# Re-ordering the seam between attention and state-space stage, and handing a block's floor from VectorE to ScalarE

## The chip, the core and the metric

One core of a Trainium2 chip runs the whole kernel in one launch. The metric is the device time of the kernel in microseconds (us). Engines are called by their short names where rows are meant: PE (TensorE), DVE (VectorE), ACT (ScalarE), POOL (GpSimd), SP (SyncE, which here only issues transfers).

## What is computed

Input `x` has 8 sequences of 512 rows and 256 columns. Layer 0 is attention with 16 heads and rotary positions (residual added), then a mixture of 16 experts with capacity 320. Layer 1, the stage in question, is a Mamba block followed by a linear layer whose input and weight are rounded to a 6-bit grid in groups of 32:

```python
xz = in_proj(x); x, z = split(xz)            # 512 inner channels
u = silu(conv4(x) + b)
dt_low, B, C = split(x_proj(u))
delta = softplus(dt_proj(dt_low) + dt_b)     # step sizes
dA = exp(delta * A); dBu = delta * B * u     # 16 states a channel
h = dA * h + dBu; y = sum(h * C)             # along 512 positions
out = out_proj((y + u * D) * silu(z))
scale = max(max|block of 32| / 7.5, tiny)    # grid of the linear layer
```

## The kernel before, in words

`route_block` chooses experts, `attend_block` does attention and the experts for one sequence after another, and `mix_block` does layer 1. All engines meet at a barrier between two of these; the **seam** here is the stretch from the barrier ahead of `mix_block` to its first scans.

In `mix_block` a **block** is one sequence (b, or f while it is being prepared, 0 to 7). Its work is 32 **steps** (n counts them over all blocks, q within one), eight to each of four chunks c of 128 channels. A step has two halves m = 2n and 2n + 1. For each half ACT writes the decays exp(delta * A) into one of five banks of PSUM (`decay`, L1447), POOL writes the drives of both halves to one of eight places in `work` (`drive`, L1325), DVE runs the recurrence in the bank (`scan`, L1554) and then multiplies the state by C (`read`, L1560), and PE sums the states of two steps (`sum_states`, L1657). So DVE's order is scan, read, scan, read, and ACT and POOL can be at most some steps ahead of it.

Step sizes reach the decays through memory: ACT takes delta out of PSUM (`take_dt`, L1410 and L1411), then softplus as an exponential (L1415) and a logarithm (L1419); POOL finishes them (`scale_input`, L1310 to L1314); SP stores them (`store_inputs`, L1214) and loads them back spread to 128 partitions (`load_inputs`, four transfers, L1224; the first two let the first step begin, the other two the second). B and C come the same way (`store_rows` L1202, `load_quad` L1209).

While block b is scanned, block f = b + 1 is prepared: each part stands at a fixed step, by the tables `PE_AT`, `ACT_AT`, `DVE_AT`, `POOL_AT` (steps counted from the start of block f - 1's steps, negative ones before it). On DVE these parts are the `statistics` and `aggregate` of the normalisation (L1517, L1524), `block_max` (L1531), the largest magnitude in each group of 32, and `block_scale` (L1535 floors it, L1537 takes its reciprocal). Everything that DVE does for them stands between two scans.

Block 0's front part runs inside `attend_block`. What is left of it at the seam (step sizes, z, the transposed constants, the linear layer's weight) and the normalising of block 1 run before the loop over steps.

## Time and profile before

| | us |
|---|---|
| median of 3 runs (lowest to highest) | 2017.42 (2014.82 to 2017.91) |
| the profiled execution: its own time | 2016.76 |
| its span in the trace | 2015.0 |
| barrier ahead of `mix_block` | 1044.6 |
| first scan starts | 1073.80 |
| last scan starts | 2003.2 |

Times inside the trace count from the span's start. In the rows further down an arrow in brackets gives the idle time before an instruction and what ended it. "L1554" is a line of the kernel before.

### The profile page before, as it was taken

Reading aid. Unit: us, or ns where it says so; the run is one execution under the profiler, and the core shown is the slowest. Engines: PE = TensorE matmul, PEld = TensorE weight load, DVE = VectorE, ACT = ScalarE, POOL = GpSimd, SP = SyncE. Lnnn points to the kernel's source line nnn. Section 1 sums busy time; section 2 is a strip of 40 time slices with the busy share of each in tenths; the row PEclk is TensorE's granted clock in tenths of the full one; section 3 lists DMA queues with packets and bytes.
Section 4 is the critical chain, followed back from the end, with each engine's and each line's share of the span. In section 5 each row is a group of like instructions: output and inputs, shape, how many; then the busy total and the mean of one; then the engine's idle time right before and its main releaser. Section 6 shows DMA issues by size and latency. Waiting matters only on the chain. (4 is left out here: it accounts for less than half of the span.)

```text
span 2015.0 us, 22043 instructions
## 1 busy us (share of the span) xinstructions
PE 1669.7 (83%) x6616; PEld 744.9 (37%) x6616; DVE 1510.4 (75%) x2254; ACT 1001.1 (50%) x1524; POOL 893.5 (44%) x662
## 2 busy tenths in 40 slices
PE   7399999999999999999978578798887878878466
PEld 7262534436253443525223123333332233323132
DVE  6436464564546466454748999999999999999998
ACT  3125435252533425253465756656575665657542
POOL 2610000000000000000339888888879888786963
PEclk9998989899898989989888688898878889788777
DMA  5573542526364252636225152333415233341520
GB/s 193 198 118 107 84 142 47 96 99 105 106 92 133 55 116 70 106 104 105 91 85 195 56 165 95 125 112 127 149 54 188 95 126 113 119 145 44 177 94 11
DMA packets 103331, 223.83 MB, mean 111 GB/s; under 512 B 12913, under 2 KB 65266, under 8 KB 99554
## 3 DMA queue, kind: packets, MB, share of 16 engines
q1 hardware_dynamic: 100194, 214.70, 38.4%
q0 software_dynamic: 3072, 8.37, 1.3%
q8 instruction: 28, 0.46, 0.1%
q14 instruction: 37, 0.30, 0.0%
HBM read 169.57 MB, written 53.48 MB: 111 GB/s over the span
## 5 line engine op out<-in xcount | busy, mean ns | idle before, releaser
L1325 POOL TENSOR_TENSOR work<-rep,bc 128x1024 f32<-128x1024 f32 x256 | 597.0, 2358 | 141.5 <-PE ps L1657 140.3
L1554 DVE TENSOR_TENSOR_SCAN ps<-ps,work 128x512 f32<-128x512 f32 x512 | 623.8, 1218 | 8.3 <-POOL work L1325 8.3
L1447 ACT ACTIVATE ps<-rep,a_neg 128x512 f32<-128x512 f32 x512 | 347.3, 689 | 335.0 <-DVE work L1560 333.5
L832 DVE TENSOR_REDUCE m<-ps 128x1 f32<-128x512 f32 x512 | 328.4, 686 | 162.1 <-PE ps L967 159.2
L719 ACT ACTIVATE prob<-ps 128x1024 f32<-128x1024 f32 x256 | 257.6, 1021 | 236.8 <-PE ps L991 235.1
L1560 DVE TENSOR_TENSOR work<-ps,bc 128x512 f32<-128x512 f32 x512 | 344.5, 673 | 0.0
L637 POOL TENSOR_TENSOR m_parts<-m,nil 128x16 bf16<-128x16 f32 x32 | 7.1, 222 | 589.5 <-DVE m L832 589.5
L1657 PE MATMUL ps<-work,pick 128*32 128x512 f32 x1024 | 165.1, 723 | 92.8 <-DVE work L1560 92.7
L1632 PE MATMUL ps<-xn_sb,front_w 128*128 128x512 f32 (+1 forms) x448 | 216.3, 637 | 26.3 <-ACT xn_sb L1381 26.3
L967 PE MATMUL ps<-k_st,q_st 96*128 96x512 bf16 x512 | 202.2, 440 | 31.7 <-DVE m L832 24.8
L991 PE MATMUL ps<-q_st,k_st 99*128 99x512 bf16 x512 | 168.9, 428 | 0.6
L933 PE MATMUL ps<-rows_t,front_w 128*128 128x320 f32 x512 | 149.4, 440 | 4.3 <-ACT rows_t L697 4.3
L1002 PE MATMUL ps<-prob,v 128*32 128x512 f32 x1024 | 149.2, 657 | 0.1
L1632 PEld LDWEIGHTS ps<-xn_sb,front_w 128*128 128x128 f32 x448 | 88.1, 203 | 159.6 <-issue 122.4
L967 PEld LDWEIGHTS ps<-k_st,q_st 96*128 96x128 bf16 x512 | 50.4, 101 | 209.7 <-DVE m L832 165.7
L942 PE MATMUL ps<-front_w,hid 128*128 128x256 f32 x512 | 120.8, 384 | 6.0 <-ACT hid_rest L701 6.0
L653 POOL TENSOR_TENSOR att<-att,x_res 128x1024 f32<-128x1024 f32 x8 | 18.8, 2347 | 236.3 <-DVE att L817 236.3
L804 DVE COPY e_out<-ps 128x256 f32<-128x256 f32 x32 | 12.0, 417 | 143.8 <-PE ps L942 143.8
L700 ACT ACTIVATE hid<-ps 128x256 f32<-128x256 f32 x128 | 49.2, 384 | 129.9 <-PE ps L933 129.9
L933 PEld LDWEIGHTS ps<-rows_t,front_w 128*128 128x128 f32 x512 | 97.4, 193 | 41.3 <-ACT rows_t L697 4.7
L942 PEld LDWEIGHTS ps<-front_w,hid 128*128 128x128 f32 x512 | 95.1, 189 | 27.4 <-ACT hid_rest L701 11.3
L1657 PEld LDWEIGHTS ps<-work,pick 128*32 128x32 f32 x1024 | 21.7, 116 | 199.2 <-DVE work L1560 156.0
(206 smaller groups left out, 1995.4 us busy)
## 6 DMA issues: line engine op xcount, KB each, us to landing
rep<-rep_rows SPq DMA_DIRECT2D x128, 512.0 KB, 6.2
front_w<-in_w SPq DMA_DIRECT2D x32, 1024.0 KB, 8.5
bc<-bc_rows SPq DMA_DIRECT2D x32, 512.0 KB, 4.7
rep_rows<-inputs SPq DMA_DIRECT2D x32, 512.0 KB, 5.4
qk_parts<-parts SPq DMA_DIRECT2D x96, 128.0 KB
q_st<-qk_parts SPq DMA_DIRECT2D x96, 128.0 KB, 10.5
k_st<-qk_parts SPq DMA_DIRECT2D x96, 128.0 KB, 11.5
dispatch<-zeros SPq DMA_DIRECT2D x4, 1280.0 KB, 10.6
```

The lines of the kernel that those rows point to most:

```text
L719: nc.scalar.activation(prob[:, n % PB, :, :], ps[:, ST[n % 2]:ST[n % 2] + 2, :], ACT.Exp, scale=SCALE).then_inc(prob_ready, 1)
L832: nc.vector.tensor_reduce(m[:, g % 2, qt, 2 * pair + i:2 * pair + i + 1], ps[:, S0 + i, :], AX.X, ALU.max).then_inc(s_reduced, 1)
L933: x = nc.tensor.matmul(ps[:, HIDE[i] + h % 2, 0:CAP], w1[:, i, k, h * P:(h + 1) * P], rows_t[:, k, :], start=(k == 0), stop=(k == KD - 1))
L942: x = nc.tensor.matmul(ps[:, E_OUT[i], j * DM:(j + 1) * DM], hid[:, h, j * P:(j + 1) * P], w2[:, i, h, :], start=(h == 0), stop=(h == HC - 1))
L967: nc.tensor.matmul(ps[:, S0 + i, :], q_st[0:STACK, h, qt * P:(qt + 1) * P], k_st[0:STACK, h, :], start=True, stop=True).then_inc(s_done, 1)
L991: x = nc.tensor.matmul(ps[:, ST[n % 2] + i, :], k_st[0:STACK + MROWS, h, kt * P:(kt + 1) * P], q_st[0:STACK + MROWS, h, :], start=True, st ...
L1325: nc.gpsimd.tensor_tensor(work[:, n % WS, :, :], rep[:, g % RS, 2 * h:2 * h + 2, 1, :], bc[:, k, 0, :].unsqueeze(1).broadcast_to([P, 2, SE ...
L1447: nc.scalar.activation(state(m), rep[:, g % RS, 2 * h + i, 0, :], ACT.Exp, scale=a_neg[:, c, 2 * h + i, k:k + 1]).then_inc(decay_ready, 1)
L1554: nc.vector.tensor_tensor_scan(state(m), state(m), work[:, n % WS, i, :], 0.0, ALU.mult, ALU.add).then_inc(state_ready, 1)
L1560: nc.vector.tensor_tensor(work[:, n % WS, i, :], state(m), bc[:, k, 1, :], ALU.mult).then_inc(read_ready, 1)
L1632: x = nc.tensor.matmul(ps[:, bank, s:], in_x[:, k, TAPS - 1 - s, c * P:(c + 1) * P], xn_t[:, k, 0:SEQ - s], start=(s == 0 and k == 0), sto ...
L1657: x = nc.tensor.matmul(ps[j * CH:(j + 1) * CH, YB, :], pick[:, :], work[:, n % WS, i, :], start=False, stop=(n % PER_CHUNK >= PER_CHUNK - 2))
```

## The change

It has three parts. **At the seam** the step sizes of chunk 0 go through exponential and logarithm alone, before those of the other three; SP stores B and C's rows first, stores chunk 0's inputs between the second and third load of B and C, and loads the linear layer's weight early under a semaphore of its own; POOL does `scale_input` of chunk 0 first, that of chunk 1 next, and those of chunks 2 and 3 inside the loop after steps 8 and 12; DVE quantises the weight and prepares the taps before the statistics of block 1; the silu of block 0's z (`first_z`, in banks 5 and 4 for its last two chunks) moves behind the decays of step 1, and the normalising of block 1 behind those of step 2. **For block 1** most parts of the preparation stand three steps later (`late`). **In every block** the floor of the group maxima moves from one DVE `tensor_scalar` to three ACT instructions (`floor_max`, step 2), `block_scale` waits for them and stands at step 2 in place of 1, and the statistics stand one step later. The tests `at == X_AT[...]` of block 1's other parts are changed like those shown.

```diff
-Z_FIRST = (6, 7, 0, 1)
+Z_FIRST = (6, 7, 5, 4)
...
-ACT_AT = {"weigh": -15, "normalise": -3, "turned": (0, 0), "x": (4, 6, 8, 10), "round": 5, "silu_u": 11, "quant": (12, 12), "rows": 14,
+ACT_AT = {"weigh": -15, "normalise": -3, "turned": (0, 0), "floor": 2, "x": (4, 6, 8, 10), "round": 5, "silu_u": 11, "quant": (12, 12), "rows": 14,
           "dt": (16, 16, 18, 18), "softplus": 20, "z": (26, 27, 29, 30), "silu_z": 31}
-DVE_AT = {"max": 0, "statistics": -11}
+DVE_AT = {"max": 0, "scale": 2, "statistics": -10}
...
+FIRST_LATE, FIRST_Z, FIRST_ROOT, FIRST_INPUT = 3, 1, 2, (0, 0, 8, 12)
...
+        def late(f):
+            return FIRST_LATE if f == 1 else 0
...
-                    sp.wait_ge(bc_stored, f * 16 + 16)
+                    if f:
+                        sp.wait_ge(bc_stored, f * 16 + 16)
...
+                store_rows(0)
+                sp.dma_start(fw_raw, io["fw"].rearrange("(t p) c -> p t c", p=P)).then_inc(w_loaded, 16)
                 sp.dma_start(a_neg[:, :, :, :], io["a_log"]).then_inc(a_loaded, 16)
...
                 sp.wait_ge(sb["x1_stored"], BATCH * 16)
-                store_rows(0)
+                sp.wait_ge(bc_stored, 16)
                 for k in range(QUADS):
+                    if k == 2:
+                        store_inputs(0, 0)
                     load_quad(0, k)
-                for c in range(DC):
-                    store_inputs(0, c)
-                    if c == 0:
-                        load_inputs(0, 0)
+                load_inputs(0, 0)
                 for b in range(BATCH + 1):
                     if b < BATCH:
                         for c in range(1, DC):
+                            if b == 0:
+                                store_inputs(0, c)
                             load_inputs(b, c)
...
-                        pool.wait_ge(log_ready, f + 1)
+                    if f == 0:
+                        pool.wait_ge(log_ready, min(c, 1) + 1)
+                    elif c == 0:
+                        pool.wait_ge(log_ready, f + 2)
...
-                pool.drain()
+                scale_input(0, 0)
                 add_experts(1)
-                root(1)
-                for c in range(DC):
-                    pool.drain()
-                    scale_input(0, c)
+                scale_input(0, 1)
                 pool.wait_ge(taps_ready, 1)
                 for n in range(BATCH * PIECES):
                     drive(n // PIECES, n % PIECES)
+                    if n == FIRST_ROOT:
+                        root(1)
+                    for c in range(2, DC):
+                        if n == FIRST_INPUT[c]:
+                            pool.drain()
+                            scale_input(0, c)
...
-                        if at == POOL_AT["down"]:
+                        if at - late(f) == POOL_AT["down"]:
...
+                def floor_max(f):
+                    act.wait_ge(max_ready, f)
+                    nc.scalar.activation(absmax[:, :, 0], absmax[:, :, 0], ACT.Copy, scale=GRID_UNIT / GRID_MAX)
+                    act.drain()
+                    nc.scalar.activation(absmax[:, :, 0], absmax[:, :, 0], ACT.Relu, bias=floor[:, 0:1])
+                    act.drain()
+                    nc.scalar.activation(absmax[:, :, 0], absmax[:, :, 0], ACT.Identity, bias=floor[:, 1:2]).then_inc(max_floored, 1)
...
-                def exponents(f):
+                def exponents(f, c0=0):
+                    cs = slice(c0, DC) if f or c0 else slice(0, 1)
                     act.drain()
-                    nc.scalar.activation(du, du, ACT.Exp, scale=-1.0)
-
-                def softplus(f):
+                    nc.scalar.activation(du[:, cs, :], du[:, cs, :], ACT.Exp, scale=-1.0)
+
+                def softplus(f, c0=0):
+                    cs = slice(c0, DC) if f or c0 else slice(0, 1)
                     act.drain()
-                    nc.scalar.activation(du, du, ACT.Ln, bias=1.0).then_inc(log_ready, 1)
+                    nc.scalar.activation(du[:, cs, :], du[:, cs, :], ACT.Ln, bias=1.0).then_inc(log_ready, 1)
...
-                for c in range(DC):
+                def first_z():
+                    for c in range(DC):
+                        act.wait_ge(z_done, c + 1)
+                        nc.scalar.activation(sz[:, 0, c, :], ps[:, Z_FIRST[c], :], ACT.Silu).then_inc(z_taken, 1)
+                    act.drain()
+
+                act.wait_ge(set_up, 1)
+                nc.scalar.activation(idle[:, :], idle[:, :], ACT.Exp)
+                take_dt(0, 0, DT_FIRST[0])
+                exponents(0)
+                softplus(0)
+                for c in range(1, DC):
                     take_dt(0, c, DT_FIRST[c])
                 act.wait_ge(a_loaded, 16)
                 nc.scalar.activation(a_neg[:, :, :, :], a_neg[:, :, :, :], ACT.Exp).then_inc(a_exp, 1)
-                exponents(0)
-                softplus(0)
+                exponents(0, 1)
+                softplus(0, 1)
                 for k in range(KD):
...
+                act.wait_ge(w_turned, 1)
+                nc.scalar.activation(fw_t[:, :, :], ps[:, W_FIRST, :].rearrange("p (k d) -> p k d", d=DM), ACT.Copy).then_inc(w_copied, 1)
...
-                for c in range(DC):
-                    act.wait_ge(z_done, c + 1)
-                    nc.scalar.activation(sz[:, 0, c, :], ps[:, Z_FIRST[c], :], ACT.Silu).then_inc(z_taken, 1)
-                act.wait_ge(w_turned, 1)
-                nc.scalar.activation(fw_t[:, :, :], ps[:, W_FIRST, :].rearrange("p (k d) -> p k d", d=DM), ACT.Copy).then_inc(w_copied, 1)
-                normalise(1)
                 act.wait_ge(a_ready, 1)
                 nc.scalar.activation(idle[:, :], idle[:, :], ACT.Exp)
                 act.drain()
                 for n in range(BATCH * PIECES):
                     b, q = n // PIECES, n % PIECES
                     decay(b, q)
+                    if n == FIRST_Z:
+                        first_z()
+                    if n == FIRST_Z + 1:
+                        normalise(1)
...
-                            if at == ACT_AT["turned"][k]:
+                            if at - late(f) == ACT_AT["turned"][k]:
...
-                        if at == ACT_AT["round"]:
+                        if at - late(f) == ACT_AT["floor"]:
+                            floor_max(f)
...
-                    nc.vector.tensor_reduce(absmax[:, :, 0], blocks(xn[:, :, :]), AX.X, ALU.max, apply_absolute_value=True)
+                    nc.vector.tensor_reduce(absmax[:, :, 0], blocks(xn[:, :, :]), AX.X, ALU.max, apply_absolute_value=True).then_inc(max_ready, 1)
 
                 def block_scale(f):
-                    dve.drain()
-                    nc.vector.tensor_scalar(absmax[:, :, 0], absmax[:, :, 0], GRID_UNIT / GRID_MAX, GRID_UNIT * 1e-30, ALU.mult, ALU.max)
-                    dve.drain()
+                    dve.wait_ge(max_floored, f)
                     nc.vector.reciprocal(inv_scale[:, :], absmax[:, :, 0]).then_inc(scale_ready, 1)
...
+                quantise_weights()
+                tap_weights()
+                dve.wait_ge(a_exp, 1)
+
+                nc.vector.tensor_scalar(a_neg[:, :, :, :], a_neg[:, :, :, :], -1.0, -1e-30, ALU.mult, ALU.min).then_inc(a_ready, 1)
                 statistics(1)
                 aggregate(1)
-                dve.wait_ge(a_exp, 1)
-
-                nc.vector.tensor_scalar(a_neg[:, :, :, :], a_neg[:, :, :, :], -1.0, -1e-30, ALU.mult, ALU.min).then_inc(a_ready, 1)
-                tap_weights()
-                quantise_weights()
...
-                        if at == DVE_AT["max"]:
+                        if at - late(f) == DVE_AT["max"]:
                             block_max(f)
-                        if at == DVE_AT["max"] + 1:
+                        if at - late(f) == DVE_AT["scale"]:
                             block_scale(f)
...
                         pe.wait_ge(y_ready, b * DC + c)
+                    else:
+                        pe.wait_ge(z_taken, DC)
...
+                turn_weights()
                 pe.wait_ge(const_loaded, CONSTS * 16)
...
-                turn_weights()
...
-                pe.wait_ge(xn_ready, 2)
-                for k in range(KD):
-                    turn(k, TB[k], xt_done)
...
-                            if at == PE_AT["turn_x"][k]:
+                            if at == (PE_AT["turn_x"][k] if f > 1 else FIRST_LATE):
...
-                            if at == PE_AT["x"][c]:
+                            if at - late(f) == PE_AT["x"][c]:
```

The first place is SP's queue at the seam. Before, from the second constant on:

```order
L1232 DMA in_z<-in_in_proj_t 128x2x512
L1232 DMA d_par<-in_d_param 128x4
L1232 DMA sz<-in_fw 128x2x256
L1232 DMA pick<-in_pick 128x32
L1232 DMA out_w<-in_out_proj_t 128x1024
L1232 DMA front_rows_w<-in_fbias 1x256
L1202 DMA bc_rows<-front_x_rows 32x512 [waits front_rows_copied,x1_stored]
L1209 DMA bc<-bc_rows 128x1x1024 [waits bc_stored]
L1209 DMA bc<-bc_rows 128x1x1024 x3
L1214 DMA rep_rows<-inputs 128x1024 [waits du_ready]
L1224 DMA rep<-rep_rows 128x1x1024 [waits rep_stored_0]
```

And in the changed kernel, from the barrier on:

```order
L1210 DMA bc_rows<-front_x_rows 32x512 [waits front_rows_copied]
L1237 DMA sz<-in_fw 128x2x256
L1238 DMA a_neg<-in_a_log 128x64
L1243 DMA work<-in_conv_w 128x2048
L1243 DMA in_z<-in_in_proj_t 128x2x512
L1243 DMA d_par<-in_d_param 128x4
L1243 DMA pick<-in_pick 128x32
L1243 DMA out_w<-in_out_proj_t 128x1024
L1243 DMA front_rows_w<-in_fbias 1x256
L1218 DMA bc<-bc_rows 128x1x1024 [waits bc_stored,x1_stored]
L1218 DMA bc<-bc_rows 128x1x1024
L1223 DMA rep_rows<-inputs 128x1024 [waits du_ready]
```

The store of B and C's rows moved from behind all constants to the front of the queue, and the store of the first inputs from behind four loads of B and C to behind two.

The second place is ACT's queue ahead of the first decays (`ps<-rep,a_neg`). Before, from the silu of z on:

```order
L1464 ACT_TABLE_LOAD
L1464 ACTIVATE sz<-ps 128x512 [waits z_done] x4
L1466 ACTIVATE fw_t<-ps 128x512 [waits w_turned]
L1376 ACTIVATE xn_sb<-xn_sb,front_shift,front_rstd 128x256 [waits quant_turned,front_rstd_ready]
L1376 ACTIVATE xn_sb<-xn_sb,front_shift,front_rstd 128x256 x3
L1469 ACT_TABLE_LOAD
L1469 ACTIVATE idle<-idle 128x1 [waits a_ready]
L1447 ACTIVATE ps<-rep,a_neg 128x512 [waits rep_loaded_0_0]
L1447 ACTIVATE ps<-rep,a_neg 128x512
L1381 ACTIVATE xn_sb<-ps 128x512 [waits front_xt_done] x2
L1447 ACTIVATE ps<-rep,a_neg 128x512 [waits rep_loaded_0_1]
```

And in the changed kernel, from the copy of the linear layer's weight on:

```order
L1499 ACTIVATE fw_t<-ps 128x512 [waits w_turned]
L1502 ACTIVATE d_diag<-ident_sb,d_par 128x128 [waits const_loaded3]
L1502 ACTIVATE d_diag<-ident_sb,d_par 128x128 x3
L1505 ACT_TABLE_LOAD
L1505 ACTIVATE idle<-idle 128x1 [waits a_ready]
L1476 ACTIVATE ps<-rep,a_neg 128x512 [waits rep_loaded_0_0]
L1476 ACTIVATE ps<-rep,a_neg 128x512
L1476 ACTIVATE ps<-rep,a_neg 128x512 [waits rep_loaded_0_1]
L1476 ACTIVATE ps<-rep,a_neg 128x512
L1482 ACT_TABLE_LOAD
L1482 ACTIVATE sz<-ps 128x512 [waits z_done] x4
L1476 ACT_TABLE_LOAD
```

The silu of z with its table load and the normalising (`xn_sb<-xn_sb,front_shift,front_rstd`) moved from ahead of the first decays to between those of step 1 and step 2, and of step 2 and step 3; one more table load stands behind the silu.

The third place is DVE's queue around block 1's maximum and scale; a scan is called SCALAR_TENSOR_TENSOR here. Before, from the first scan on:

```order
L1554 SCALAR_TENSOR_TENSOR ps<-ps,work 128x512 [waits drive_ready,decay_ready]
L1531 TENSOR_REDUCE front_absmax<-xn_sb 128x32 [waits front_quant_ready,front_xn_ready]
L1554 SCALAR_TENSOR_TENSOR ps<-ps,work 128x512 [waits decay_ready]
L1560 TENSOR_TENSOR work<-ps,bc 128x512 [waits state_ready]
L1554 SCALAR_TENSOR_TENSOR ps<-ps,work 128x512 [waits drive_ready,decay_ready]
L1535 TENSOR_SCALAR front_absmax<-front_absmax 128x32
L1537 RECIPROCAL front_inv_scale<-front_absmax 128x32
L1560 TENSOR_TENSOR work<-ps,bc 128x512 [waits state_ready]
```

And in the changed kernel, from the scan of step 3 on:

```order
L1594 SCALAR_TENSOR_TENSOR ps<-ps,work 128x512 [waits drive_ready,decay_ready]
L1573 TENSOR_REDUCE front_absmax<-xn_sb 128x32 [waits front_quant_ready,front_xn_ready]
L1600 TENSOR_TENSOR work<-ps,bc 128x512 [waits state_ready]
L1594 SCALAR_TENSOR_TENSOR ps<-ps,work 128x512 [waits decay_ready]
L1600 TENSOR_TENSOR work<-ps,bc 128x512 [waits state_ready]
L1594 SCALAR_TENSOR_TENSOR ps<-ps,work 128x512 [waits drive_ready,decay_ready]
L1600 TENSOR_TENSOR work<-ps,bc 128x512 [waits state_ready]
L1594 SCALAR_TENSOR_TENSOR ps<-ps,work 128x512 [waits decay_ready]
L1600 TENSOR_TENSOR work<-ps,bc 128x512 [waits state_ready]
L1594 SCALAR_TENSOR_TENSOR ps<-ps,work 128x512 [waits drive_ready,decay_ready]
L1577 RECIPROCAL front_inv_scale<-front_absmax 128x32 [waits max_floored]
L1600 TENSOR_TENSOR work<-ps,bc 128x512 [waits state_ready]
```

The floor (`TENSOR_SCALAR front_absmax`) is gone from between a scan and its read, the reciprocal now waits for ACT, and maximum and reciprocal lie two steps apart in place of one.

## Rows read from the trace of the kernel before

**Rows 1.** The page: span, and VectorE in 40 slices of it.

```profile
span 2015.0 us, 22043 instructions
...
DVE  6436464564546466454748999999999999999998
```

**Rows 2.** Groups by line and shape, VectorE, 1074–2006 us (busy, mean ns; idle before).

```profile
L1554 DVE TENSOR_TENSOR_SCAN ps<-ps,work 128x512 f32<-128x512 f32 x512 | 623.8, 1218 | 8.3 <-POOL work L1325 8.3
...
L1517 DVE BATCH_NORM_STATS2 front_stats<-xn_sb 128x6 f32<-128x256 f32 x24 | 8.4, 413 | 3.6 <-POOL xn_sb L1280 3.6
...
L1535 DVE TENSOR_SCALAR front_absmax<-front_absmax 128x32 f32<-128x32 f32 x7 | 8.1, 1162 | 0.7
...
L1537 DVE RECIPROCAL front_inv_scale<-front_absmax 128x32 f32<-128x32 f32 x7 | 2.5, 354 | 0.5
```

**Rows 3.** Timeline of VectorE from the seam on (start us, us).

```profile
1054.29 5.71 DVE L1546 TENSOR_TENSOR front_w<-front_w,work 128x1024 f32<-128x1024 f32 x4 [1.16 <-DMA front_rows_w<-in_fbias]
...
1073.80 1.23 DVE L1554 TENSOR_TENSOR_SCAN ps<-ps,work 128x512 f32<-128x512 f32 x1 [8.30 <-POOL work L1325]
...
1079.08 1.90 DVE L1535 TENSOR_SCALAR front_absmax<-front_absmax 128x32 f32<-128x32 f32 x1
...
1090.45 1.22 DVE L1554 TENSOR_TENSOR_SCAN ps<-ps,work 128x512 f32<-128x512 f32 x1
```

**Rows 4.** Timeline of ScalarE at the seam.

```profile
1045.97 0.69 ACT L1410 ACTIVATE inputs<-ps,front_dt_b 128x512 f32<-128x512 f32 x1 [1.44 <-PE ps L1644]
...
1050.72 1.28 ACT L1453 ACT_TABLE_LOAD   x1
...
1052.01 0.26 ACT L1453 ACTIVATE a_neg<-a_neg 128x64 f32<-128x64 f32 x1
...
1055.62 1.91 ACT L1419 ACTIVATE inputs<-inputs 128x2048 f32<-128x2048 f32 x1
...
1060.97 1.66 ACT L1464 ACTIVATE sz<-ps 128x512 f32<-128x512 f32 x3
...
1066.75 2.06 ACT L1376 ACTIVATE xn_sb<-xn_sb,front_shift,front_rstd 128x256 f32<-128x256 f32 x4
...
1070.94 1.30 ACT L1447 ACTIVATE ps<-rep,a_neg 128x512 f32<-128x512 f32 x2 [0.62 <-DMA rep<-rep_rows]
...
1073.94 1.91 ACT L1447 ACTIVATE ps<-rep,a_neg 128x512 f32<-128x512 f32 x3 [0.70 <-DMA rep<-rep_rows]
```

**Rows 5.** Timeline of GpSimd at the seam.

```profile
1057.61 1.31 POOL L1310 TENSOR_TENSOR inputs<-inputs 128x512 f32<-128x512 f32 x1 [0.89 <-ACT inputs L1419]
...
1071.35 2.34 POOL L1325 TENSOR_TENSOR work<-rep,bc 128x1024 f32<-128x1024 f32 x1
```

**Rows 6.** Timeline of SP at the seam.

```profile
1061.38 0.35 SPq L1214 DMA_DIRECT2D rep_rows<-inputs  x1
...
1064.70 2.46 SPq L1224 DMA_DIRECT2D rep<-rep_rows  x4
```

**Rows 7.** Windows (length; busy; PEclk, DMA share, GB/s).

```profile
1048.00:1074.00 26.00, 14.76 (x39) 7.55 (x38) 12.82 (x20) 21.41 (x33) 20.84 (x20) 0.71 0.76 266
...
1066.00:1069.00 3.00, 0.27 (x3) 0.08 (x2) 0.00 (x0) 2.73 (x6) 2.58 (x4) 1.00 1.00 311
```

**Rows 8.** Timeline of all engines around the scale of block 3.

```profile
1297.77 16.23 POOL L1325 TENSOR_TENSOR work<-rep,bc 128x1024 f32<-128x1024 f32 x7
...
1311.63 0.69 ACT L1447 ACTIVATE ps<-rep,a_neg 128x512 f32<-128x512 f32 x1 [1.03 <-DVE work L1560]
...
1312.82 1.22 DVE L1535 TENSOR_SCALAR front_absmax<-front_absmax 128x32 f32<-128x32 f32 x1
```

**Rows 9.** Timeline of all engines around the scale of block 2.

```profile
1196.01 0.18 DVE L1535 TENSOR_SCALAR front_absmax<-front_absmax 128x32 f32<-128x32 f32 x1
...
1198.08 4.68 POOL L1325 TENSOR_TENSOR work<-rep,bc 128x1024 f32<-128x1024 f32 x2 [3.56 <-PE ps L1657]
```

**Rows 10.** One line's instructions, L1537 (ns: min/median/max).

```profile
L1537 DVE RECIPROCAL front_inv_scale<-front_absmax x7: 352/353/355, 1081.1 to 1784.7; 128x32 f32<-128x32 f32 x7
```

41 lines of the change are left out of this document (24 added, 17 removed).

## The prediction

> **What bounds the kernel now.** I read the page's slices first, then VectorE by line, then the timelines of the seam, then two blocks in close view. The slices show VectorE at 40 to 60% until the seam and at 90% or more from there to the end [rows 1]. The groups by line say what that means: 512 scans, 8.3 us of idle before them, all of it ahead of the first one [rows 2]. In the loop a scan follows a scan without waiting: from the first to the ninth, 1073.80 to 1090.45, each scan with its read takes about 1.72 us once the maximum and the scale (1079.08) are taken out [rows 3]. So two rules hold. What VectorE does or waits for between two scans costs its full length; what moves the first scan moves the end by as much, if nothing starves VectorE behind it.
>
> Ahead of the first scan a chain decides. On ScalarE the logarithm of all four chunks ends at 1057.5 [rows 4]; GpSimd then takes 1057.61 to about 1061.3 for chunk 0 [rows 5]; SP stores at 1061.38, and the loads wait for it until 1064.70, 3.3 us [rows 6]. The first two loads have landed by 1070.9, the other two by 1073.9, since ScalarE's decays begin then with a wait on them [rows 4]. GpSimd's drive of 2.34 us from 1071.35 [rows 5] ends at 1073.7, and the scan starts at 1073.80 [rows 3]. ScalarE was ready at 1070.3 (its decay at 1070.94 had waited 0.62) and GpSimd, by the start of its drive, only at 1071.3: a gain needs all three.
>
> **The seam.** The same bytes move in both kernels. In 1048 to 1074 the queues carried 266 GB/s at a share of 0.76, in 1066 to 1069 311 GB/s at 1.00 [rows 7]. 26 us at 266 GB/s are 6.9 MB; at 311 GB/s they take 22.2 us, so 3.8 us can be won at that rate. The second half's 1 MB took 3.0 us, about 350 GB/s [rows 4]; by that rate it would be 6.2 us. Between them I take 4.5 us.
>
> Can the chain follow? Chunk 0 alone: its two take-outs of 0.57 us each end near 1047.2 (they stand first now too, 1045.97); its exponential and logarithm are a quarter of 1.91 us and some fixed time, say 0.65 us each, with one table load of 1.28 us between them [rows 4]: 1050 in place of 1057.5. GpSimd's 3.3 to 3.7 us give 1053.5. The store of B and C's rows stands ahead of all constants, so their loads can go as soon as `x1_stored` lets them, and the store of the first inputs is issued near 1054 in place of 1061.38. The store no longer comes last; what comes last is the queue itself, with the constants, four loads of B and C (2 MB) and four of the inputs (2 MB). I put the first half at 1066.3 (from 1065.5 to 1069) and the second at 1069.6.
>
> ScalarE: from 1050 six take-outs (3.5), a table load, the constant's exponential (0.3), 1536 elements (1.5), a load, 1.5, the copies of the weight, its turned form and the diagonals (2.8, of which 2.2 lie between the logarithm's end and the silu's table load), a load and 0.2 [rows 4]. With 3.84 for the three loads that is 13.6 us, 1063.6; with gaps 1064.2. It comes out before the loads because the silu (1.28 + 4 times 0.55) and the normalising (2.1) moved behind. GpSimd has done chunk 0 and 1 and the addition near 1062.5, since chunks 2 and 3 moved into the loop; a chunk took (1071.2 - 1061.3) / 3 = 3.3 us [rows 5]. The taps of 5.71 us on VectorE [rows 3] stand behind the weight's quantising now, whose input comes early; I estimate their end near 1060, no limit either. First scan = 1066.3 + 0.1 + 2.34 + 0.1 = 1068.85: **4.95 us earlier**.
>
> Some is given back. `first_z` stands between the decays of steps 1 and 2: a load 1.28, four silus 2.2, a load 1.28 [rows 4], 4.8 us in which no decay comes. VectorE has the decays of four halves to work on, 6.9 us from the first scan on. Those of halves 2 and 3 wait for the second loads, 1069.6; behind them and `first_z` that of half 4 comes at 1069.6 + 1.3 + 0.1 + 4.8 + 0.7 = 1076.5 or a little more. VectorE wants it at 1068.85 + 6.9 = 1075.7, hence a wait of 0.8 to 1.5, taken as 1.15. GpSimd's second drive needs 2.34 us behind the loads at 1069.6, done 1072.2, where VectorE wants it at 1072.3 less what slips: 0.35 at most. Together **1.5 us lost**. Normalising at step 2 (2.06 us) and the copy at step 3 (1.0, the space between the first two rows of decays) [rows 4] are covered by banks that are ahead by then, since ScalarE needs 1.3 us a step and VectorE 3.43. Uncovered they would cost the 3.1. `scale_input` in the loop takes 3.3 us after steps 8 and 12; GpSimd needs 2.34 of every 3.43 us and has 8 steps to gather a lead, so nothing.
>
> **The floor.** The seven `tensor_scalar` on 32 elements took 8.1 us, 1162 ns each [rows 2]. Two close views say why: in block 3 it started at 1312.82 and ended at 1314.04, with GpSimd's drive ending at 1314.00 [rows 8]; in block 2 GpSimd had been idle for 3.56 us before 1198.08, and the same instruction took 0.18 us [rows 9]. It waited for a running GpSimd instruction. The Trainium skill, "SBUF — State Buffer", section "Who interferes with whom", says that `tensor_scalar` can take a port pair shared with GpSimd and that the loser blocks for the whole instruction; the trace agrees. By the same page an instruction with at most one SBUF input outside that mode does not contend.
>
> What stays is the reciprocal: 352, 353, 355 ns, never more [rows 10], so it doesn't wait for GpSimd. Removed: 8.1 us busy, and of the idle before it and before the reciprocal 0.7 + 0.5 [rows 2]: **9.3 us won** over seven blocks. On ScalarE come three instructions on 32 elements; none is in the trace of before. The nearest is one on 64 elements, 0.26 us [rows 4]; with a drain behind each I take about 1 us. It is hidden: in block 3 ScalarE's decay at 1311.63 had waited 1.03 us for a bank that VectorE freed [rows 8], so ScalarE is five halves, 8 us, ahead. The maximum stands two steps ahead of the reciprocal now, and ScalarE does its part behind the decay of step 2, which it ends some 3 us before VectorE comes to the reciprocal. Uncovered it would cost 1 us a block, 7 us.
>
> **The statistics** one step (3.43 us) later: VectorE waited 3.6 us for GpSimd's addition ahead of them, over six blocks 0.6 each [rows 2], less than 3.43. Later by a step the addition is done: **3.6 us won**. What follows (GpSimd's root, ScalarE's normalising, eight steps behind) has room. **Block 1 three steps later** costs nothing: PE and ScalarE do the same things with the same waits, and the one end that comes near is GpSimd's first input of block 1, which would wait about 3 us for the logarithm and has a lead of some 6.
>
> **Sum.** 4.95 - 1.5 + 9.3 + 3.6 = 16.35 us. The profiled execution took 2016.76, 0.66 under the median of 2017.42 and inside the three runs' spread. 2016.76 - 16.35 = **2000.4 us** (2001.1 by the median). A measurement of this kernel can tell 0.2%, 4 us, from no change.
>
> **The rivals.**
> A, the forecast: 0.61. Its own range is 1997 to 2004: seam from +1 to +6, the hand-over between +7 and +9.3.
> B, the reciprocal inherits the wait: ScalarE's floor comes late by about what `tensor_scalar` cost, a new idle time in the old one's place, and only some 1.2 of the 9.3 us stay. 16.35 - 8.1 = 8.25, 2008.5 us. Against it speaks ScalarE's lead [rows 8]. 0.12.
> C, the first scan is no sooner: the queue is as full as before and its order only moves the gap, or ScalarE with two more table loads is ready at 1070 again. 16.35 - 4.95 = 11.4, 2005.4 us. For it: before, ScalarE was ready only 0.6 us ahead of the loads and GpSimd 0.4 behind them, so the loads alone gain little. 0.14. In this trace a table load of 1.28 us begins right behind the instruction before it (1050.72) and the next starts right at its end (1052.01) [rows 4]. The Trainium skill, "ScalarE: Activation LUTs", section "What ACT_TABLE_LOAD costs", counts a drain of about 1.38 us on top of 1.28. By it five loads would bring ScalarE to 1071, `first_z` would cost 2.8 us more, and the time would be about 2008; the trace does not show such a drain, and I give this 0.02 inside C's 0.14.
> D, the queue has more to give: the first inputs come before 1064, and ScalarE at 1064.2 sets the start. First scan at 1064.2 + 0.65 (decay), or GpSimd at 1066.7: 2.1 us more, 18.5 in all, 1998.3 us. 0.07.
> E, slower: ScalarE comes to `floor_max` late in every block, since it waits there in order for VectorE's maximum and all decays are queued behind it. Seven blocks must lose (16.35 + 4) / 7 = 2.9 us each; with a lead of 3 us that needs ScalarE 6 us later than I see, or banks that are empty. Against it speaks the full set of banks that ScalarE had to wait for [rows 8]. At a miss of 3.5 us each the time is 2025. 0.03.
> F, the parts cancel or nothing moves: the seam's gain is given back by `first_z` and B holds as well, 2013.5 to 2017.5. 0.03.
>
> The range of 8 in 10 takes in A, D and C, 0.82, and since each case has some 3 us to either side from the terms' own bounds, it reaches up to B as well: 1996 to 2009. Faster by over 0.2%: A, B, C and D, 0.94; the same: F, 0.03; slower: E, 0.03.
>
> **What the next profile shows.** First scan near 1068.9 (right between 1067 and 1070; at 1073 C). One wait of about 1 us on ScalarE's decay before the fifth scan. No `tensor_scalar` on the maxima; the reciprocal, seven times 0.35 us, with idle under 1 us in sum before it (8 us is B). Statistics without GpSimd's addition ahead of them. ScalarE's floor instructions 0.2 to 0.3 us each. Idle of VectorE on GpSimd's drive only at the first steps: a wait in step 9 to 16 or 24 to 32 would mean that an input moved into the loop, or block 1's lateness, is not covered.

## The result, and the profile after

The changed kernel takes 2004.95 us (median of 5 runs, 2000.23 to 2005.94) where the kernel before takes 2016.6 (5 runs). The ratio is 0.9942, with an interval of 0.9929 to 0.9956: 11.7 us less. The forecast was 2000.4, its range 1996 to 2009: direction and range held, and of the 16.35 us forecast some 12 came. The profiled execution has a span of 2004.1 us. Executions over 1.5% slower than the fastest of their kernel (2415.74, 3059.16 and 6689.77 us, one each of the kernel before, e2 and e5) are left out of all ratios.

```profile
span 2004.1 us, 22068 instructions
...
DVE  6436465554647456464748999999999999999998
```

One thing must be known before traces are compared. The code ahead of the barrier is the same in all kernels here, but the barrier comes at 1044.8 us in the profiled execution of before, at 1046.5 in that of the changed kernel, and between 1040.9 and 1050.8 over all the traces below. So I count from GpSimd's first instruction behind it (in the kernel before it starts at 1044.80) to the first scan, and from there to the last scan; the second count is called the loop. GpSimd's timeline in the changed kernel shows it:

```profile
1046.49 0.10 POOL L1342 MEMSET idle<- 128x1 f32 x1 [5.41 <-POOLq L474]
```

In these counts the kernel before has 29.0 + 929.35 and the changed kernel 24.4 + 921.95: 12.0 us less. Behind the last scan it is 0.6 less (11.85 and 11.26 us to the end of the span).

The groups of VectorE by line and shape, from the seam on, stand against [rows 2]:

```profile
L1594 DVE TENSOR_TENSOR_SCAN ps<-ps,work 128x512 f32<-128x512 f32 x512 | 623.7, 1218 | 6.6 <-POOL work L1339 4.7 <-ACT ps L1476 2.0
L1600 DVE TENSOR_TENSOR work<-ps,bc 128x512 f32<-128x512 f32 x512 | 344.0, 672 | 0.0
L1608 DVE TENSOR_TENSOR sz<-ps,sz 128x512 f32<-128x512 f32 x32 | 21.6, 676 | 4.8 <-PE ps L1700 4.8
L1573 DVE TENSOR_REDUCE front_absmax<-xn_sb 128x32 f32<-128x1024 f32 x7 | 8.4, 1194 | 0.0
L1559 DVE BATCH_NORM_STATS2 front_stats<-xn_sb 128x6 f32<-128x256 f32 x24 | 8.3, 406 | 0.0
L1577 DVE RECIPROCAL front_inv_scale<-front_absmax 128x32 f32<-128x32 f32 x7 | 2.4, 336 | 0.0
```

The `tensor_scalar` on the maxima is gone, the reciprocal has no idle time ahead of it, and the statistics (L1559) have none either. These are the two terms that came out as forecast. New is idle time ahead of the **gate**, 4.8 us on PE (before, 2.06 us, all at the last gate behind the last scan), and 2.0 us ahead of scans on ScalarE. The gate (L1608) is VectorE's product of a chunk's summed states with silu(z); it stands in the third step of the next chunk, so the first one is in step 10, and needs PE's last sum of the chunk. VectorE's timeline says where the waits are:

```profile
1070.89 2.35 DVE L1594 TENSOR_TENSOR_SCAN ps<-ps,work 128x512 f32<-128x512 f32 x2 [4.24 <-POOL work L1339]
...
1074.24 1.23 DVE L1594 TENSOR_TENSOR_SCAN ps<-ps,work 128x512 f32<-128x512 f32 x1 [0.43 <-POOL work L1339]
...
1078.51 1.23 DVE L1594 TENSOR_TENSOR_SCAN ps<-ps,work 128x512 f32<-128x512 f32 x1 [0.74 <-ACT ps L1476]
...
1110.92 0.69 DVE L1608 TENSOR_TENSOR sz<-ps,sz 128x512 f32<-128x512 f32 x1 [2.39 <-PE ps L1700]
...
1139.20 1.23 DVE L1594 TENSOR_TENSOR_SCAN ps<-ps,work 128x512 f32<-128x512 f32 x1 [1.24 <-ACT ps L1476]
```

And later on, in the blocks behind:

```profile
1574.19 0.69 DVE L1608 TENSOR_TENSOR sz<-ps,sz 128x512 f32<-128x512 f32 x1 [0.30 <-PE ps L1700]
```

```profile
1806.07 0.69 DVE L1608 TENSOR_TENSOR sz<-ps,sz 128x512 f32<-128x512 f32 x1 [0.52 <-PE ps L1700]
```

The seam's own waits were forecast (0.35 on the drive, here 0.43; 1.15 on the decay, here 0.74). The 2.39 us at the first gate and the 1.24 us at a decay of step 18 (the expectations below call it step 20) were not, nor were three small ones of 0.30, 0.44 and 0.52 us at the first gate of blocks 4 to 6. (1.19 us more stand at the last gate, behind the last scan.) The seam itself, by SP and ScalarE, against [rows 4, 6]:

```profile
1055.25 0.34 SPq L1223 DMA_DIRECT2D rep_rows<-inputs  x1
...
1061.62 2.45 SPq L1233 DMA_DIRECT2D rep<-rep_rows  x4
```

```profile
1063.90 1.28 ACT L1505 ACT_TABLE_LOAD   x1
1065.20 0.20 ACT L1505 ACTIVATE idle<-idle 128x1 f32<-128x1 f32 x1
1068.34 1.30 ACT L1476 ACTIVATE ps<-rep,a_neg 128x512 f32<-128x512 f32 x2 [2.94 <-DMA rep<-rep_rows]
1071.75 1.30 ACT L1476 ACTIVATE ps<-rep,a_neg 128x512 f32<-128x512 f32 x2 [2.11 <-DMA rep<-rep_rows]
```

The store was issued 8.8 us behind the barrier (in the kernel before 16.6), but took 6.4 us until the loads that wait for it were issued, where it took 3.3 before; this is called its landing below. ScalarE was ready 18.9 us behind the barrier and waited 2.94 us for the inputs. In ScalarE's part of the seam five table loads stand, each 1.28 us, with the next instruction right at its end (1063.90 + 1.28, next 1065.20).

ScalarE's floor instructions in block 3 stand between decays, where ScalarE had waited for VectorE:

```profile
1310.26 0.69 ACT L1476 ACTIVATE ps<-rep,a_neg 128x512 f32<-128x512 f32 x1 [1.03 <-DVE work L1600]
...
1311.57 0.33 ACT L1419 ACTIVATE front_absmax<-front_absmax,floor 128x32 f32<-128x32 f32 x1
```

What stands ahead of the gate's wait is on PE: the matmuls of the **taps** (L1673; the input projection of block 1, done once for each tap of its convolution) and the sums of states (L1700). In the changed kernel:

```profile
1084.90 8.88 PE L1673 MATMUL ps<-xn_sb,front_w 128*128 128x512 f32 x16 [0.69 <-ACT xn_sb L1400]
...
1102.74 7.11 PE L1673 MATMUL ps<-xn_sb,front_w 128*128 128x512 f32 x16
1109.79 1.06 PE L1700 MATMUL ps<-work,pick 128*32 128x512 f32 x8
```

Sixteen matmuls of the taps, 7.11 us, of which the last eight belong to step 8, lie ahead of the sum that the gate at 1110.92 needs. In the kernel before, the taps began at 1073.29, the first gate waited for nothing, and PE's timeline shows:

```profile
1073.29 13.56 PE L1632 MATMUL ps<-xn_sb,front_w 128*128 128x512 f32 x24 [2.57 <-ACT xn_sb L1381]
```

PE's clock has a part in it too. In the changed kernel PE ran nothing for 9.97 us ahead of 1076.58, and in 1072 to 1088 its granted clock was 0.50, which is 1.2 GHz; it was back at 1.00 (2.4 GHz) from 1090. The windows of the first and the last sixteen taps above (length; busy; PEclk, DMA share, GB/s):

```profile
1084.90:1093.78 8.88, 8.88 (x20) 3.69 (x24) 8.88 (x12) 5.38 (x11) 8.62 (x5) 0.80 0.00 0
1102.74:1109.80 7.06, 7.06 (x22) 2.97 (x19) 5.79 (x7) 4.60 (x8) 6.64 (x6) 1.00 0.39 154
```

The same sixteen matmuls took 8.88 us at a clock of 0.80 and 7.11 us at 1.00, so 1.8 us of PE's lateness come with the clock. The kernel before lost as much and more (its 24 taps took 13.56 us at a clock of 0.78), but there the gate left PE the time. With the 1.8 us alone gone, 0.6 us of the 2.39 us would be left, by an estimate from these two windows; no run changes the clock by itself.

ScalarE and GpSimd around the gather of block 2's expert rows, in the changed kernel; ScalarE's instruction **weighs** the gathered rows (multiplies them by their gate values):

```profile
1136.88 1.71 ACT L1386 ACTIVATE xn_sb<-xn_sb,front_gate_cur 128x256 f32<-128x256 f32 x4 [3.89 <-DMA xn_sb<-expert_out,front_slot_cur]
1138.49 1.89 ACT L1476 ACTIVATE ps<-rep,a_neg 128x512 f32<-128x512 f32 x3
```

```profile
1123.56 1.08 POOL L1285 DMA_INDIRECT xn_sb<-expert_out,front_slot_cur  x1 [0.81 <-issue]
```

And GpSimd in the kernel before:

```profile
1120.08 1.08 POOL L1273 DMA_INDIRECT xn_sb<-expert_out,front_slot_cur  x1 [0.81 <-issue]
```

GpSimd began the gather 52.7 us behind the first scan; in the kernel before it was 46.3 us (1120.08 - 1073.80). ScalarE waited 3.89 us in its queue for what it brings, with the decays of the next steps behind it.

### The profile page after: what moved, and what is told of

It reads as the page before. It is cut to its first block and busy times, and to the rows that moved or that the text cites. A ratio compares the mean times of both kernels' runs of the same rounds, so it can differ in the third digit from the quotient of the medians.

```text
span 2004.1 us, 22068 instructions
## 1 busy us (share of the span) xinstructions
PE 1667.2 (83%) x6616; PEld 747.3 (37%) x6616; DVE 1500.8 (75%) x2247; ACT 1008.5 (50%) x1551; POOL 892.0 (45%) x664
## 5 line engine op out<-in xcount | busy, mean ns | idle before, releaser
L1600 DVE TENSOR_TENSOR work<-ps,bc 128x512 f32<-128x512 f32 x512 | 344.0, 672 | 0.0
L1673 PE MATMUL ps<-xn_sb,front_w 128*128 128x512 f32 (+1 forms) x448 | 216.3, 637 | 24.6 <-ACT xn_sb L1400 24.6
L1700 PE MATMUL ps<-work,pick 128*32 128x512 f32 x1024 | 164.4, 720 | 85.7 <-DVE work L1600 85.5
L992 PE MATMUL ps<-q_st,k_st 99*128 99x512 bf16 x512 | 168.7, 428 | 0.6
L1673 PEld LDWEIGHTS ps<-xn_sb,front_w 128*128 128x128 f32 x448 | 88.3, 204 | 157.8 <-issue 121.7
L1700 PEld LDWEIGHTS ps<-work,pick 128*32 128x32 f32 x1024 | 21.6, 116 | 190.2 <-DVE work L1600 150.8
## 6 DMA issues: line engine op xcount, KB each, us to landing
q_st<-qk_parts SPq DMA_DIRECT2D x96, 128.0 KB, 10.7
```

Source lines behind the costliest of these rows:

```text
L992: x = nc.tensor.matmul(ps[:, ST[n % 2] + i, :], k_st[0:STACK + MROWS, h, kt * P:(kt + 1) * P], q_st[0:STACK + MROWS, h, :], start=True, st ...
L1600: nc.vector.tensor_tensor(work[:, n % WS, i, :], state(m), bc[:, k, 1, :], ALU.mult).then_inc(read_ready, 1)
L1673: x = nc.tensor.matmul(ps[:, bank, s:], in_x[:, k, TAPS - 1 - s, c * P:(c + 1) * P], xn_t[:, k, 0:SEQ - s], start=(s == 0 and k == 0), sto ...
L1700: x = nc.tensor.matmul(ps[j * CH:(j + 1) * CH, YB, :], pick[:, :], work[:, n % WS, i, :], start=False, stop=(n % PER_CHUNK >= PER_CHUNK - 2))
```

## The experiments

Each ratio is to the kernel before, timed in the same rounds, five or more. "Barrier to scan" and "loop" are the two counts from above, in us, from one profiled execution of each kernel; their sum is what I go by, and the ratio with its interval says whether the times agree. An unchanged seam repeats only roughly: the six traces that have the changed kernel's seam show 22.9 to 24.5 us. How well a loop repeats is not known, as each kernel was profiled once. In e2, e4 and e7 the profiled execution took 4 to 7 us longer than any other of its kernel in the ratio, with a late barrier (1049.3, 1050.7 and 1050.8 us); for e2 and e4 the ratio says more is won than the counts do (e2 7.9 us and 4.9, e4 12.9 and 8.7).

| run | ratio (interval) | barrier to scan | loop | sum |
|---|---|---|---|---|
| before | 1 | 29.0 | 929.35 | 958.4 |
| changed kernel | 0.9942 (0.9929 to 0.9956) | 24.4 | 921.95 | 946.4 |
| e1 floor alone | 0.9957 (0.9944 to 0.9970) | 28.95 | 918.68 | 947.6 |
| e2 statistics alone | 0.9961 (0.9948 to 0.9974) | 29.0 | 924.48 | 953.5 |
| e3 seam and late block 1 | 0.9990 (0.9982 to 0.9999) | 23.75 | 933.15 | 956.9 |
| e4 gate later | 0.9936 (0.9920 to 0.9951) | 24.5 | 925.25 | 949.7 |
| e5 late block 1 alone | 0.9991 (0.9981 to 1.0001) | 29.4 | 929.52 | 958.9 |
| e6 weighing later | 0.9926 (0.9910 to 0.9942) | 23.3 | 922.65 | 945.9 |
| e7 floor on VectorE, other form | 0.9936 (0.9919 to 0.9953) | 22.9 | 923.63 | 946.5 |
| e8 two loads later | 0.9941 (0.9925 to 0.9957) | 23.8 | 922.05 | 945.9 |
| e9 floor and statistics, no seam | 0.9942 (0.9927 to 0.9957) | 28.9 | 917.41 | 946.3 |
| e10 sum first in every chunk | 1.0020 (1.0011 to 1.0029) | 23.5 | 940.50 | 964.0 |
| e11 e10 and earlier store | 1.0010 (1.0001 to 1.0019) | 22.3 | 941.65 | 964.0 |
| e12 e11, sum first once | 0.9909 (0.9893 to 0.9925) | 22.5 | 917.38 | 939.9 |

**e1, the floor alone, on the kernel before.**

```diff
+                        if at == ACT_AT["floor"]:
+                            floor_max(f)
...
-                    nc.vector.tensor_scalar(absmax[:, :, 0], absmax[:, :, 0], GRID_UNIT / GRID_MAX, GRID_UNIT * 1e-30, ALU.mult, ALU.max)
+                    dve.wait_ge(max_floored, f)
...
-                        if at == DVE_AT["max"] + 1:
+                        if at == DVE_AT["max"] + 2:
```

> The kernel before with the floor alone moved: VectorE's `tensor_scalar` on the maxima is gone, ScalarE does the floor at step 2 in three instructions, the reciprocal stands at step 2. Theory (the forecast's term): 9.3 us less, since the 8.1 us busy and 1.2 us idle go and nothing comes in their place; ratio near 0.9954. Rival (PE bound behind a faster VectorE): what VectorE gives up in the first steps of a block brings it to the gate of step 10 sooner than PE has summed, some 0.3 to 0.5 us of wait appears there in three to five blocks, and 7.5 to 8.5 us are won. Rival B of the forecast (the reciprocal inherits the wait): 1 to 2 us won. The reciprocal's idle time and the gate's idle time on PE tell them apart.

The loop is 10.7 us shorter than before. No gate in the loop waits on PE, and the reciprocal has no idle time:

```profile
L1581 DVE TENSOR_TENSOR sz<-ps,sz 128x512 f32<-128x512 f32 x32 | 21.5, 673 | 2.1 <-PE ps L1670 2.1
L1532 DVE BATCH_NORM_STATS2 front_stats<-xn_sb 128x6 f32<-128x256 f32 x24 | 8.4, 413 | 3.1 <-POOL xn_sb L1283 3.1
...
L1550 DVE RECIPROCAL front_inv_scale<-front_absmax 128x32 f32<-128x32 f32 x7 | 2.4, 338 | 0.0
```

The gate's 2.1 us are the last one, which stood there before too. Of the 10.7 us, 9.4 are the forecast's term; the statistics' wait fell from 3.6 to 3.1, and reads and scans took some 0.9 us less in sum. The rival with PE at the gates falls for this run, and rival B of the forecast falls for good.

**e2, the statistics alone**: one number, -11 to -10, on the kernel before.

> The kernel before with the statistics alone one step later. Theory: the 3.6 us that VectorE waited for GpSimd's addition ahead of the statistics go and nothing else moves; ratio near 0.9982. Rival: the wait goes but shows again at the normalising or at the next scan, since GpSimd's root and ScalarE's normalising come later by the same step; ratio 0.999 to 1.000. VectorE's idle time in the loop tells.

Behind the first scan VectorE waits for no other engine any more, and the loop is 4.9 us shorter: the 3.6, `tensor_scalar`s that took 7.4 us in place of 8.1, and some 0.6 spread over the rest. The wait shows up nowhere else, so the rival falls and the forecast's term stands by the trace. The timing says more, 5.2 to 10.5 us less by its interval; what the difference is stays open.

**e3, the seam and the late steps alone**: the changed kernel with VectorE's old floor and the old place of the statistics.

```diff
-DVE_AT = {"max": 0, "scale": 2, "statistics": -10}
+DVE_AT = {"max": 0, "scale": 1, "statistics": -11}
...
-                        if at - late(f) == ACT_AT["floor"]:
-                            floor_max(f)
...
-                    dve.wait_ge(max_floored, f)
+                    dve.drain()
+                    nc.vector.tensor_scalar(absmax[:, :, 0], absmax[:, :, 0], GRID_UNIT / GRID_MAX, GRID_UNIT * 1e-30, ALU.mult, ALU.max)
+                    dve.drain()
```

> The changed kernel with VectorE's own floor again (at step 1 behind the maximum) and the statistics one step sooner again: the seam and the three late steps of block 1 alone. The forecast's terms for them give 3.45 us less than before (ratio 0.9983). Theory from the changed kernel's trace: the first scan comes 4.6 us sooner behind the barrier, 0.43 us of wait for a drive and 0.74 for a decay follow, then 2.4 us at the first gate on PE and 1.2 at a decay of step 20, so 0 us to 1 us are left (ratio 0.9995 to 1.000), and some 0.9 at the end. Rival: the gate's and the decay's waits come only with a VectorE that has lost its `tensor_scalar`; then they are absent here and 3.5 us are won.

Of the 5.2 us won ahead of the first scan 3.8 are given back behind it: 0.94 on the drive, 0.74 on the decay, 1.22 at step 18, 0.16 at the first gate, the rest on `tensor_scalar`s that now took 8.8 us in place of 8.1. VectorE's timeline:

```profile
1072.34 1.23 DVE L1594 TENSOR_TENSOR_SCAN ps<-ps,work 128x512 f32<-128x512 f32 x1 [0.94 <-POOL work L1339]
...
1076.61 1.23 DVE L1594 TENSOR_TENSOR_SCAN ps<-ps,work 128x512 f32<-128x512 f32 x1 [0.74 <-ACT ps L1476]
...
1109.21 0.69 DVE L1608 TENSOR_TENSOR sz<-ps,sz 128x512 f32<-128x512 f32 x1 [0.16 <-PE ps L1700]
...
1137.47 1.23 DVE L1594 TENSOR_TENSOR_SCAN ps<-ps,work 128x512 f32<-128x512 f32 x1 [1.22 <-ACT ps L1476]
```

The two counts together are 1.5 us less than before, the timing says 2.0 (0.2 to 3.6 by the interval), where the forecast's terms gave 3.45. So the wait at step 18 belongs to the seam. The one at the gate is small here (0.16): VectorE's `tensor_scalar` of block 1 took 2.13 us ahead of it. The 2.39 us need the seam's late PE and the VectorE that has lost its `tensor_scalar`, together.

**e5, late block 1 alone, on the kernel before** (`FIRST_LATE = 3` in the tests of the tables; normalising and turning stay ahead of the loop).

> The kernel before with one edit: most parts of block 1's preparation stand three steps later, the normalising and turning of block 1 stay ahead of the loop, floor and statistics as before. The forecast put this at nothing: ratio 1.000. Theory from the changed kernel's trace: the 64 matmuls of block 1's taps now reach into the step at which VectorE's first gate waits for PE's sum, so 1 to 2.4 us of wait appear there, and up to 1.2 us at a decay of step 20; ratio 1.0005 to 1.0018. If both waits are absent here, they come from the later start of PE at the seam.

Neither wait is there, and the loop is 929.52 against 929.35 (the statistics' wait was 0.8 us longer, the `tensor_scalar`s 0.8 shorter). On the kernel before the lateness costs nothing, as the forecast had it. VectorE has its old floor here, so this is no test of a faster VectorE. But PE can be compared. The sum that the first gate needs, in this run and then in the kernel before:

```profile
1104.79 1.06 PE L1661 MATMUL ps<-work,pick 128*32 128x512 f32 x8
```

```profile
1108.33 1.06 PE L1657 MATMUL ps<-work,pick 128*32 128x512 f32 x8
```

Both end 35.6 us behind the first scan (at 1070.26 and 1073.80). In the changed kernel the sum ends 40.0 us behind it (1070.89), where VectorE wanted it at 37.6.

**e4, every gate one step later**: `GATE = 3` in place of 2, on the changed kernel.

> The changed kernel with VectorE's gate one step later in every chunk (step 11 in place of 10 of the first chunk, and so on). Theory (PE's sum of the chunk comes too late for the gate, because VectorE now reaches step 10 sooner than PE has worked off the taps): the waits of 2.39, 0.30, 0.44 and 0.52 us on PE ahead of the gate are gone, 3.4 to 3.7 us less than the changed kernel, ratio to the kernel before near 0.9925. Rival: PE's next sum has to wait for the gate to empty the bank, so PE idles a step more and GpSimd's drives or the tail pay; the waits move and the ratio stays near 0.994.

The waits on PE at the gates are gone from the loop, as the theory says, and in this trace the loop is 3.3 us longer than the changed kernel's all the same. The timing doesn't tell the two apart (0.9936 and 0.9942). In their place VectorE waits ten times for ScalarE or GpSimd behind the seam's own wait, the longest again behind the gather, in step 18:

```profile
1142.00 1.23 DVE L1594 TENSOR_TENSOR_SCAN ps<-ps,work 128x512 f32<-128x512 f32 x1 [2.58 <-ACT ps L1476]
```

```profile
1139.69 1.70 ACT L1386 ACTIVATE xn_sb<-xn_sb,front_gate_cur 128x256 f32<-128x256 f32 x4 [3.68 <-DMA xn_sb<-expert_out,front_slot_cur]
```

The rival holds in that the waits move: PE's next chunk must wait for the gate that frees the bank (PE's idle time ahead of the seed, the first matmul of a chunk's sum, rose from 31.5 to 87.3 us). That ScalarE and GpSimd are late because PE is, is read from the trace only.

**e6, the weighing one step later**: `"weigh": -14` in place of -15, on the changed kernel.

> The changed kernel with ScalarE's weighing of the gathered expert rows one step later. In the changed kernel ScalarE waited 3.9 us for the gather ahead of it in step 17, and VectorE then 1.24 us for a decay. Theory (the gather is late, since GpSimd has the two inputs of block 0 in the loop; ScalarE's queue holds the decays behind it): VectorE's wait of 1.24 us near 1139 is gone, ratio 0.0006 lower than that of the changed kernel, which timing alone can hardly tell, the trace can. Rival: the wait comes from ScalarE's total work there, then it stays or moves to the next step, and GpSimd's addition waits for the weighing.

The wait at step 18 is gone, so its cause is ScalarE's queue behind the gather. The loop is no shorter: the first gate waits 2.76 us in place of 2.39, and the first gates of blocks 1 to 6 wait 0.16 to 0.48. The sum of both counts is 945.9 against 946.4.

**e7, the floor on VectorE in another form**, on the changed kernel; ScalarE's three instructions are gone.

```diff
-                    dve.wait_ge(max_floored, f)
+                    dve.drain()
+                    nc.vector.tensor_scalar(absmax[:, :, 0], absmax[:, :, 0], GRID_UNIT / GRID_MAX, GRID_UNIT * 1e-30, ALU.mult, ALU.max, accum_out=idle[:, 0:1])
+                    dve.drain()
```

> The changed kernel with the floor back on VectorE at step 2 right ahead of the reciprocal, as a `tensor_scalar` that also writes its accumulated sum to a scratch column; ScalarE's three instructions and the hand-over are gone. Theory (the `tensor_scalar` of before was long only because it wanted the port pair that GpSimd held, and this form doesn't): about 0.2 us each instead of 1.16, with GpSimd's drives running; the loop is 2 to 2.6 us longer than the changed kernel's where no other wait absorbs it. Rival (any VectorE instruction of this kind meets GpSimd, or the handing on to the reciprocal is the cost): 1.1 to 1.3 us each again, 8 to 10 us longer.

The line's instructions (ns: min/median/max):

```profile
L1575 DVE TENSOR_SCALAR_CACHE_REDUCE front_absmax<-front_absmax x7: 186/186/191, 1094.3 to 1782.7; 128x32 f32<-128x32 f32 x7
L1575 DVE DVE_READ_ACCUMULATOR front_absmax<-front_absmax x7: 81/83/86, 1094.4 to 1782.8; 128x1 f32 x7
```

186 to 191 ns, seven times, each time with a drive of GpSimd running, where the plain form took 1162 on average [rows 2]. So the old floor cost little by its own work; what it cost was the wait for GpSimd, and it need not have left VectorE for that. The Trainium skill, "SBUF — State Buffer", section "Who interferes with whom", says that `tensor_scalar` can want the pair of ports shared with GpSimd, except in the form that also writes its accumulator: the trace agrees, 1162 ns against 187. The loop is 1.7 us longer than with ScalarE's floor; the edit puts 3.2 us on VectorE (1.3 + 0.6 busy, 1.3 idle), and the gates' three small waits, 1.3 us, take up part of it. By the timing it is the changed kernel's equal (0.9936 and 0.9942).

**e8, the third and fourth load of B and C behind the first inputs**, on the changed kernel.

```diff
-                for k in range(QUADS):
-                    if k == 2:
-                        store_inputs(0, 0)
+                for k in range(2):
                     load_quad(0, k)
+                store_inputs(0, 0)
                 load_inputs(0, 0)
+                for k in range(2, QUADS):
+                    load_quad(0, k)
```

> The changed kernel with the third and fourth load of B and C moved behind the four loads of the first inputs (they are read from step 4 on). Theory (the queue's bytes set the first scan: 1 MB less ahead of the first inputs at 325 to 385 GB/s): the first inputs land 2.6 to 3.1 us sooner, but GpSimd is busy with the input of chunk 1 until 1065.05 (18.6 us behind the barrier), and its drive takes 2.34; the first scan comes 21.1 to 21.4 us behind the barrier in place of 24.4, ratio near 0.9927. Rival (the chain store, wait, load sets it, at a latency that the bytes do not change): first scan 24 us behind the barrier, ratio unchanged; or VectorE waits in step 4 for GpSimd, which waits for the third load.

```profile
1053.23 0.34 SPq L1223 DMA_DIRECT2D rep_rows<-inputs  x1
1059.62 2.46 SPq L1233 DMA_DIRECT2D rep<-rep_rows  x4
```

The store again took 6.4 us to land, so loads behind it do not matter to it. The first inputs landed 6.1 us behind their issue (6.7 in the changed kernel), and the first scan stands 23.8 us behind the barrier, inside the spread of the changed seam. The theory wanted 21.1 to 21.4 and falls: it is not all of the queue's bytes that count.

**e9, floor and statistics without the seam**: e1 with the one number of e2.

> The kernel before with the floor on ScalarE and the statistics one step later together, and none of the seam: no chunk 0 alone, no moved silu, no late steps of block 1. The two parts alone left a loop (first to last scan) of 918.7 and 924.5 us in place of 929.35. Theory (the gains add, and the seam's earlier first scan is given back behind it): loop 915 to 916 us, first scan 29 us behind the barrier, barrier to last scan 944.5, which is 1.5 to 2 us less than the changed kernel's 946.35; ratio 0.993 to 0.994. Rival (the seam's gain is real in the end): barrier to last scan 948 to 950, since waits on PE appear at the gates here as well; ratio near 0.9955.

Barrier to last scan is 946.34, the changed kernel's 946.35, and the ratio is the same. Neither the 944.5 of the theory nor the rival's 948: behind the two parts 1.8 us of small gate waits appear (0.29 to 0.55 in blocks 3 to 6), and the first gate waits for nothing. So beside the other two parts, the seam's part of the change with the late steps is worth nothing that can be told, give or take the 1 us by which an unchanged seam repeats: it wins 4.5 us ahead of the first scan and gives as much back behind it. Without them, in e3, it was worth 1.5.

**e10, the sum that the gate needs first, and the weighing of e6.**

```diff
+                    if n and n % PER_CHUNK == 0:
+                        sum_states(n // 2 - 1)
                     for f, at in chains(n):
...
-                    if n and n % 2 == 0:
+                    if n and n % 2 == 0 and n % PER_CHUNK:
```

> The changed kernel with two edits: the last sum of a chunk, which the gate waits for, stands ahead of that step's other matmuls on PE, and ScalarE weighs the experts' rows one step later. Theory (in step 8 of block 0 this sum is queued behind eight matmuls of the taps, 3.6 us): the wait of 2.4 to 2.8 us at the first gate is gone, that of 1.24 us at step 20 too; first to last scan 918.5 to 919.5 in place of 921.95. Rival (PE is short of time over all steps since its late start): the sum finds its data no sooner or the taps end later by as much, and the wait moves to the next gate, or to ScalarE's first take-outs; loop 920.5 or more.

In block 0 both waits are gone. But the loop is 18.6 us longer. PE now waits for VectorE's reads with its other work queued behind, at the start of each chunk, and twice in each of blocks 1 to 6 VectorE waits in turn:

```profile
1186.37 1.94 PE L1700 MATMUL ps<-work,pick 128*32 128x512 f32 x8 [6.05 <-DVE work L1600]
1188.23 11.93 PE L1673 MATMUL ps<-xn_sb,front_w 128*128 128x512 f32 x24
```

```profile
1342.35 0.69 DVE L1608 TENSOR_TENSOR sz<-ps,sz 128x512 f32<-128x512 f32 x1 [1.80 <-PE ps L1700]
...
1382.50 1.23 DVE L1594 TENSOR_TENSOR_SCAN ps<-ps,work 128x512 f32<-128x512 f32 x1 [2.10 <-ACT ps L1476]
```

PE's idle time ahead of the sums is 168.7 us in place of 85.5. Theory and rival were both written for block 0 alone, and neither saw this. That the edit at the other chunks is the cause is shown by e12; the way from PE's wait to those two of VectorE is read from the trace only.

**e11, e10 with the store of the first inputs ahead of all loads of B and C.**

```diff
+                store_inputs(0, 0)
                 for k in range(2):
                     load_quad(0, k)
-                store_inputs(0, 0)
                 load_inputs(0, 0)
```

> The kernel of the run with the earlier sum, and SP's queue in another order: the store of the first inputs ahead of all four loads of B and C, then two of these, the loads of the first inputs, and the other two. Theory (the store's 6.4 us to landing are the bytes queued ahead of it, since with two loads fewer behind it nothing changed): 1 MB less ahead of it at 350 to 400 GB/s, the store lands 2.5 to 3 us sooner, the two loads of B and C fill the time, and the first scan comes 22 to 22.5 us behind the barrier in place of 23.3 to 24.4, as GpSimd is busy until 18.6 and ScalarE until 18.9. Rival (the constants still in flight set it): no change, 23.5 to 24.

```profile
1053.92 0.33 SPq L1223 DMA_DIRECT2D rep_rows<-inputs  x1
...
1056.97 2.56 SPq L1233 DMA_DIRECT2D rep<-rep_rows  x4
```

The store landed 3.05 us behind its issue in place of 5.9 in e10 and 6.4 in the changed kernel, and the first scan comes 22.3 us behind the barrier: the theory holds, what counts is what is queued ahead of the store. Not all of it is won: the first inputs now took 7.9 us from their issue to ScalarE's first decay, 6.4 in e10, so that this decay came 1.2 us sooner behind the barrier and not 2.8. In the loop the trace shows e10's waits again.

**e12, e11 with the early sum at one place**: `n == PER_CHUNK` (step 8 of block 0) in place of every chunk's start.

> As the run with the earlier store, but the sum stands ahead of the other matmuls only in step 8 of block 0; in all other chunks PE's order is the changed kernel's. Theory (the 20 us lost came from PE waiting for VectorE's reads ahead of its taps at every chunk's start, from block 2 on, and the first gate's wait is a matter of that one place): first scan 22.3 us behind the barrier, first to last scan 918 to 919 us, barrier to last scan 940.5 to 941.5 in place of the changed kernel's 946.35; ratio to the kernel before near 0.9915, below the changed kernel's. Rival (an earlier first scan is given back again, since PE's late start sets the first block): barrier to last scan 944 to 946, ratio near 0.994.

The loop is 917.38, barrier to last scan 939.9, and the ratio 0.9909: 1997.1 us against 2016.4 for the kernel before in the same rounds. It beats the changed kernel (0.9942); the two intervals, 0.9893 to 0.9925 and 0.9929 to 0.9956, do not meet. Three of e12's parts differ from the changed kernel: the store, e6's weighing and the one early sum. Behind the first scan this wait is left in the loop:

```profile
1070.55 1.23 DVE L1595 TENSOR_TENSOR_SCAN ps<-ps,work 128x512 f32<-128x512 f32 x1 [0.40 <-ACT ps L1477]
```

and 0.21, 0.35 and 0.42 us at the first gates of blocks 4 to 6. PE still does 24 matmuls of the taps in one stretch, but the sum stands ahead of them, and the gate, at 1100.48, finds it done:

```profile
1096.65 1.06 PE L1701 MATMUL ps<-work,pick 128*32 128x512 f32 x8
1097.65 10.53 PE L1674 MATMUL ps<-xn_sb,front_w 128*128 128x510 f32 x24
```

The order is not all of it. PE's granted clock was back at 1.00 here when the taps began (PE had idled 7.57 us ahead of its first matmul, not 9.97), and the first sixteen took 7.11 us, not 8.88:

```profile
1076.95:1084.06 7.11, 7.11 (x20) 3.02 (x24) 7.11 (x10) 4.64 (x10) 7.11 (x4) 1.00 0.00 0
```

Eight matmuls (3.7 us) later the sum would have ended at 1101.4, 0.9 us behind the gate. In e10, where the first sixteen took 8.80 us as in the changed kernel, the early sum was enough by itself.

## Why the forecast held, and where it was off

The measured 2004.95 lies in the range but outside the forecast's own case (1997 to 2004). It is nearest to rival C's 2005.4, and not by C's mechanism: the first scan came 4.6 us sooner. The range held because the waits that no case had, 4.9 us in sum, happen to be as large as the term that C would have lost; that is luck.

Against the profiled execution of the kernel before, the changed one is 12.6 us shorter from the barrier on, and 1.7 us of that are lost in the span by a later barrier, which is no part of the change. The terms, each as forecast and as measured:

- **First scan 4.95 us earlier.** 4.6 from the barrier (29.0 to 24.4). Right in size, partly by another way than told: the queue moved up to 408 GB/s in windows of 2 us, above the 311 to 350 assumed, but the store's landing took twice what [rows 6] showed, and e8 and e11 show that the loads ahead of the store are the cause, not the sum of bytes. ScalarE was ready 18.9 us behind the barrier, forecast 19.6. The Trainium skill, "ScalarE: Activation LUTs", section "What ACT_TABLE_LOAD costs", adds a drain of about 1.38 us to each load, and an estimate from that figure would have had ScalarE ready near 26.4. The trace does not agree: each of the five loads took 1.28 us, with the next instruction right behind it.
- **1.5 us given back at the seam.** 0.43 + 0.74 = 1.2 at the places named. Right in sum; the one on the decay was put at 1.15.
- **"`scale_input` in the loop ... so nothing."** This step failed. It looked at GpSimd's drives and not at its gather of expert rows, which began 6.4 us later, about the time of the two inputs (3.3 us each); ScalarE waited 3.9 us for it and VectorE 1.24. The forecast's own sign for this, a wait on a drive in steps 9 to 16, never came: the wait came in step 18, on a decay. e3 has the wait, e5 and e9 don't, e6 takes it away. That the two inputs made the gather late is read from the times, not shown by a run that moves them alone.
- **"Block 1 three steps later costs nothing."** True on the kernel before (e5), wrong in the change: 2.39 us at the first gate. It takes the late start of PE's taps (1084.90 in place of 1073.29) and a VectorE that comes sooner (e3: 0.16). "PE and ScalarE do the same things with the same waits" is the step that failed: PE started later, its first sixteen taps took 8.88 us at the lower clock, which it could not make up for now, as sixteen matmuls of the taps take 7.1 us where two steps of VectorE take 6.9. e10 takes the wait away by PE's order (with e6's weighing, which by itself does not). By the traces it is not the three late steps that make PE late: with them alone the sum ends 35.6 us behind the first scan, as before (e5), early enough for the 37.6 of the changed VectorE. The rest of the seam moves it to 40.0, with the taps begun 14.0 us behind the first scan and not 10.2 as in e5. How much of that is the turning, moved into the loop behind `first_z` and the normalising, no run shows alone.
- **The floor, 9.3 us.** 9.4: 8.1 busy, 1.2 idle and 17 ns less a reciprocal. Right, and e7 shows the reason. ScalarE's three instructions took 0.22, 0.33 and 0.33 us, and VectorE waited for none of them (the reciprocal's idle time is 0.0).
- **The statistics, 3.6 us.** Right, all of it.
- **Left out: PE behind a faster VectorE.** 1.26 us at the first gates of blocks 4 to 6. Absent in e1, where the statistics' wait was still there, and in e2, where the old floor was; present in e9. Once VectorE waits for nothing else, PE's taps and sums of a block's first eight steps are what it meets.

4.6 - 1.2 - 1.24 - 2.39 + 9.4 + 3.6 - 1.26 is 11.5 us; with 0.6 behind the last scan and 0.5 that the reads took less (344.5 to 344.0 us in the groups) that makes the 12.6. What e9 adds is the harder reading: the first scan's 4.6 us and the 4.8 us of waits that follow it in the first twenty steps cancel, and by these counts the whole gain is the two small edits. Rival F of the forecast had the seam's gain given back, but by `first_z`, which took 0.74 of the 4.8, and it had the floor's gain lost too.

## What to carry to other kernels

Work moved from ahead of a loop into its first steps is not hidden because the engine that does it has time on average: ask which of its queued duties comes next (a gather, a sum) and who waits for that. When the bound engine becomes faster, the one behind it with the least slack over any eight steps is the next bound; list these slacks ahead of the change, per stretch and not per block, and read PE's granted clock where it has just idled. An edit of order on an in-order engine should be made at the one place that waits: the same edit at every chunk cost 18.6 us of loop (e10), while e12, which has it at one place, has a loop 5.3 us shorter than e6, from which it differs in that and in the store; part of this is PE's clock.

## What was unexpected of the hardware

The same VectorE operation on 32 elements took 1162 ns on average in its plain form and 187 ns in the form that also sums, with a drive of GpSimd running all seven times. A 512 KB store took 2.7 to 4.0 us from its issue to that of the load that waits for it where no load of B and C was queued ahead of it (e11, e12) or the four had been issued 4 us and more before (before, e1, e2, e5, e9), and 5.7 to 6.5 us with two such loads of 512 KB right ahead (the other seven). Having run nothing for 9.97 us and then only short pieces of work for 8.3, PE took 8.88 us for sixteen matmuls of the taps, at a mean granted clock of 0.80, and 7.12 us for the next sixteen. And the same code ahead of the barrier ended at anything from 1040.9 to 1050.8 us, more than most single edits here are worth.
